# Mixture of experts: every expert over every row, or 39 routed tiles of 256 rows

## The reference, cut to what matters

```python
x = x + tanh(g_xattn[1]) * _L1_xattn_ref(ctx, _layernorm(x), ...)   # attention with 16 heads of 64, keys = x's and ctx's rows
x = x + tanh(g_ffn[1]) * _L1_ffn_ref(_layernorm(x), Wg, W1, W2, W3)

def _L1_ffn_ref(x, Wg, W1, W2, W3):            # E = 8 experts, K = 2, H = 256
    gate_out = einsum('bsd,ed->bse', x, Wg)
    top_v, top_i = top_k(gate_out, K)
    probs = softmax(top_v)
    out = zeros_like(x)
    for e in range(E):
        w_e = sum(probs * (top_i == e), axis=-1)
        h1, h2 = x @ W1[e].T, x @ W2[e].T
        out = out + ((h1 * sigmoid(h1) * h2) @ W3[e].T) * w_e[..., None]
    return out
```

## Time and profile before

| | |
|---|---|
| profiled execution, its own time | 1409.91 us |
| its span, first to last instruction | 1407.9 us |
| mean granted TensorE clock | 0.887 |
| PE, DVE, ACT, POOL busy | 1186.7, 1085.4, 931.6, 903.1 us |
| attention of layer 1 | about 475 to 1068 us |
| mixture | about 1105 to 1408 us |
| DMA, mean over the span | 26 GB/s |

### The profile page before, as it was taken

One profiled execution on the slowest core, in us unless ns is written; L12 is line 12 of the kernel. 1 busy time (PEld: TensorE's weight loads), 2 busy tenths in 40 slices (PEclk: granted clock), 3 DMA queues, 4 the chain that ended last, 5 costly groups with the idle time before them and its releaser, 6 DMA issues. The chain is left out here.

```text
span 1407.9 us, 39161 instructions
## 1 busy us (share of the span) xinstructions
PE 1186.7 (84%) x14613; PEld 889.4 (63%) x14613; DVE 1085.4 (77%) x2846; ACT 931.6 (66%) x1858; POOL 903.1 (64%) x855
## 2 busy tenths in 40 slices
PE   1578999949874699999999999999994688888887
PEld 1445777734542488888887878787873355555555
DVE  5888888867868666767767676868675799998996
ACT  0668999936655488787887878787872455454554
POOL 0250999945767366676666666666663477777778
PEclk9669555559995799999999999999997799999999
DMA  9100000001220011111111211112111000000000
GB/s 228 55 1 1 13 16 16 16 10 27 42 53 1 1 32 32 32 32 32 25 32 32 32 25 32 32 32 30 31 29 23 1 2 9 8 7 7 7 8 16
DMA packets 121437, 37.30 MB, mean 26 GB/s; under 512 B 105876, under 2 KB 119612, under 8 KB 121276
## 3 DMA queue, kind: packets, MB, share of 16 engines
q1 hardware_dynamic: 110235, 31.70, 10.8%
q10 hardware_dynamic: 11040, 3.42, 1.0%
HBM read 9.92 MB, written 2.10 MB: 9 GB/s over the span
## 5 line engine op out<-in xcount | busy, mean ns | idle before, releaser
L1178 POOL TENSOR_TENSOR attention_pl_l<-attention_probs_l,attention_ph_l 128x512 f16<-128x512 f32 x128 | 148.4, 1159 | 180.3 <-ACT attention_ph_l L1348 180.3
L1412 DVE TENSOR_REDUCE attention_negmax<-bank 128x2 f16<-128x410 f32 x256 | 137.7, 579 | 136.3 <-PE bank L1257 136.0
L1594 POOL TENSOR_TENSOR mixture_hidden_l<-mixture_hidden,mixture_hidden_h 128x512 f16<-128x512 f32 x128 | 148.4, 1160 | 74.8 <-ACT mixture_hidden_h L1681 74.8
L612 POOL TENSOR_TENSOR attention_probs_l<-attention_probs,attention_probs_h 77x512 f16<-77x512 f32 x128 | 145.5, 1153 | 52.7 <-ACT attention_probs_h L694 48.5
L1178 POOL TENSOR_TENSOR attention_pl_c<-attention_probs_c,attention_ph_c 77x512 f16<-77x512 f32 x128 | 147.8, 1155 | 0.0
L1690 ACT ACTIVATE mixture_tanh<-bank 128x512 f32<-128x512 f32 x128 | 76.4, 597 | 105.3 <-PE bank L1641 105.3
L1639 PE MATMUL bank<-mixture_xs,moeh 128*128 128x512 f16 x256 | 98.2, 383 | 32.0 <-DVE mixture_hidden L1772 32.0
L1272 PEld LDWEIGHTS bank<-identh,attention_negmax 128*128 128x128 f16 (+1 forms) x1024 | 83.3, 107 | 55.7
L1240 PE MATMUL bank<-layer_kv,ah 128*128 128x128 f16 x1024 | 108.7, 220 | 11.1 <-PEq L89 11.0
L1348 ACT ACTIVATE attention_probs_l<-bank 128x512 f32<-128x512 f32 x128 | 76.4, 597 | 56.8 <-PE bank L1272 56.8
L1268 PE MATMUL bank<-attention_th,layer_kv 128*128 128x512 f16 (+1 forms) x256 | 97.0, 379 | 14.7 <-issue 14.5
(11 more groups left out here) (323 smaller groups left out, 4788.0 us busy)
## 6 DMA issues: line engine op xcount, KB each, us to landing
X<-in_x SPq DMA_DIRECT2D x4, 512.0 KB, 9.2
out<-X SPq DMA_DIRECT2D x8, 256.0 KB, 2.3
attention_turned_h<-attention_heads_h SPq DMA_TRANSPOSE x96, 2.3
attention_turned_l<-attention_heads_l SPq DMA_TRANSPOSE x96, 2.3
ctx<-in_ctx SPq DMA_DIRECT2D x1, 1232.0 KB
setup_nat_w<-in_w SPq DMA_DIRECT2D x1, 1024.0 KB, 14.6
setup_nat_f<-in_fw ACTq DMA_DIRECT2D x2, 256.0 KB, 6.9
setup_nat_q<-in_q ACTq DMA_DIRECT2D x1, 512.0 KB, 8.3
```

What stands on the lines that cost most here:

```text
L612: pool.tensor_tensor(probs_l[:, n % SLOTS], probs[:, n % 2], probs_h[:, n % SLOTS], ALU.subtract).then_inc(p_split, 1)
L1178: last = pool.tensor_tensor(low[:, g % 2], whole[:, g % 2], high[:, g % 2], ALU.subtract)
L1412: last = dve.tensor_reduce(negmax[:, g, 2 * i:2 * i + 2], score[i], AX.X, ALU.max, negate=True)
L1594: pool.tensor_tensor(hidden_l[:, e % 4, j], hidden[:, e % 2, j], hidden_h[:, e % 4, j], ALU.subtract).then_inc(hid_lo, 1)
```

## The change

**Setup.** A DRAM tensor `tokens` of ROWS = 34560 rows of 272 fp16 (544 bytes) is written once with a blank row by one DMA that SP issues last in its setup block. POOL makes some constants more.

**Attention 1.** The routing of each batch k of four sequences is spread over later sequences, on fixed places (`ending(b, lag)` gives k where b = 4k + lag): reciprocal roots on POOL by the power function and one Newton step (lag 6 for the output, 7 for X), normed rows on ACT, a packed row of high half, low half and its number (`pay`, lag 7 to 8), four DMA transposes and one copy on SP, gates on PE (lag 9), the two largest and their indices on DVE, the choice on POOL, the rank of each row within its expert on PE (lag 10), the slot on DVE and POOL (lag 11), and then eight indirect DMAs by POOL, one per unit, that scatter 128 rows each into `tokens`. The stage runs `B + 14` turns, the last 14 without attention. DVE then makes a table of 39 tiles.

**Experts.** 39 tiles of 256 rows of one expert each. Their number is a constant: (2 * 4096 + 8 * 255) // 256. SP loads and transposes a tile from DRAM, ACT fetches the row numbers, PE, ACT and DVE work as before but with 256 rows, POOL scatters the results to `outputs` in DRAM with two indirect DMAs per tile. Then both results of each row are read back, and DVE adds them to X with their shares.

```diff
+T = 256
+ROW = 2 * 128 + 16
+TILES = (2 * B * S + E * (T - 1)) // T
+ROWS = E * B * S + (TILES - 2 * B * S // T) * T
@@ setup, sync
+            sp.wait_ge(blank_in, 1)
+            sp.dma_start(w.tokens.rearrange("(t p) r -> p t r", p=128),
+                         w.blank[:].unsqueeze(1).broadcast_to([128, ROWS // 128, ROW])).then_inc(w.cleared, 16)
@@ attention1, gpsimd
+            def row_scale(i, var, mean, eps):
+                y, z = rstd[:, i], shift[:, i]
+                link(pool.tensor_scalar(part[:], var, eps, None, ALU.add))
+                link(pool.tensor_tensor(y, part[:], power[:], ALU.pow))
+                for _ in range(1):
+                    link(pool.tensor_tensor(z, y, y, ALU.mult))
+                    link(pool.tensor_tensor(z, z, part[:], ALU.mult))
+                    link(pool.tensor_scalar(z, z, -0.5, 1.5, ALU.mult, ALU.add))
+                    link(pool.tensor_tensor(y, y, z, ALU.mult))
+                link(pool.tensor_scalar(z, mean, -1.0, None, ALU.mult))
+                return pool.tensor_tensor(z, z, y, ALU.mult)
+            def fill(k):
+                pool.wait_ge(pay_hi, k + 1)
+                pool.iota(...)
+                pool.tensor_tensor(pay[:, u, 0, :, D:2 * D], normed_x, pay[:, u, 0, :, 0:D], ALU.subtract).then_inc(pay_lo, 1)
+            def select(k):
...
+                link(pool.tensor_copy(chosen[:], index[:, :, 0:2]))
+                for i in range(2):
+                    for c in range(BATCH):
+                        last = pool.tensor_scalar(is_it[:, i, c], w.iota[:], chosen[:, c, i:i + 1], None, ALU.is_equal)
...
+            def send(k, q):
...
+                pool.indirect_dma_start(w.tokens, bass.IndirectOffsetOnAxis(ap=slot[:, u, i, c:c + 1], axis=0),
+                                        pay[:, u, i, c], None).then_inc(sent[u], 16)
@@ attention1, sync
+            def rows(k):
...
+                sp.wait_ge(pay_lo, k + 1)
+                for c in range(BATCH):
+                    sp.dma_start_transpose(rows_t[:, u, c], pay[:, u, 0, c, 0:2 * D]).then_inc(turned_x[u], 16)
...
+                sp.dma_start(pay[:, u, 1, :, 0:2 * D], pay[:, u, 0, :, 0:2 * D]).then_inc(doubled[u], 16)
@@ attention1, tensor: in project(t)
+                k = ending(t, 7)
+                if k is not None:
+                    pe.wait_ge(topped, 2 * k + 1)
+            def choose(k):
+                pe.wait_ge(turned_x[u], 16 * BATCH * (k // 2 + 1))
...                                                        # 16 matmuls of 8 columns
@@ attention1, vector
+            def top_two(k):
+                dve.wait_ge(gated, k + 1)
...
+                dve.tensor_copy(gate[:].rearrange("p c e -> p (c e)"), gates).then_inc(topped, 1)
-            def guess(k):
-            def newton(k, i):
-            def out_norm(k):
@@ experts
+            for n in range(TILES):                          # sync
+                row = sp.value_load(w.table[0:1, 0, n:n + 1], min_val=0, max_val=ROWS - T)
+                if n >= RX:
+                    sp.wait_ge(h_done, n - RX + 1)
+                sp.dma_start_transpose(xt[:, n % RX], w.tokens[bass.ds(row, T), 0:2 * D]).then_inc(x_in[n % RX], 16)
+            back = w.outputs.rearrange("(b s i) d -> s b i d", s=S, i=2)
+            for k in range(NCH):
+                sp.dma_start(both[:, k % RB], back[:, CH * k:CH * k + CH]).then_inc(both_in[k % RB], 16)
+            for n in range(TILES + LAG + 1):                # scalar
+                if n < TILES:
+                    squash(n)
+                if 1 <= n < TILES + 1:
+                    hidden_high(n - 1)
+                if n < TILES:
+                    number(n)                               # value_load and a DMA of the row numbers
+                if n >= LAG + 1:
+                    copy_out(n - LAG - 1)
+            for n in range(TILES + 1):                      # vector
+                if n < TILES:
+                    halve(n)
+                    hide(n)
+                if n >= 1:
+                    hidden_low(n - 1)
+            def send(n):                                    # gpsimd
+                pool.wait_ge(y_copied, n + 1)
+                pool.wait_ge(id_in[n % RI], 16 * (n // RI + 1))
+                for r in range(T // S):
+                    pool.indirect_dma_start(w.outputs, ..., y_rows[:, n % RY, r], None, ...).then_inc(y_out[n % RY], 16)
@@ flamingo
+                nc.clear_and_free_semaphores(w.spent)
+                nc.all_engine_barrier()
                 attention1(nc, w, bank, kv)
-            split_transposed(nc, w, bank, "split2", [...], before=row_scale(w))
-            mixture(nc, a, w, bank, xh, xl)
+        nc.clear_and_free_semaphores(w.spent)
+        nc.all_engine_barrier()
+        experts(nc, a, w, bank)
```

More of the change, by code:

```diff
@@ L1152, in attention1, with unit, ending @@
         out_p = bank[7][:, 0:D]
+        gates = bank[7][:, 128:128 + E * BATCH]
+        rank = bank[7][:, 256:256 + E * BATCH].rearrange("p (c e) -> p c e", e=E)
+        count = bank[7][:, 384:384 + E]
         LAT, CTX = slice(0, S), slice(S, KV)
         VALUES_AHEAD = 3
[L1157 to L1161, removed]
+        UNITS = B * G
+        BATCHES = B // BATCH
+        ROUTED = 14
+        def unit(n):
+            return (n // G, n % G, n // G % 2)
+        def ending(b, lag):
+            k, rest = divmod(b - lag, BATCH)
+            return k if rest == 0 and 0 <= k < BATCHES else None
         def sequences(body):
-            for b in range(B):
-                body(b, b % 2, b == 0, b == B - 1)
+            for b in range(B + ROUTED):
+                body(b)
         def batch(k):
@@ L1212, in body @@
                         add_bias(k)
[L1213 to L1216, removed]
+                    k = ending(b, 6)
+                    if k is not None and g == 0:
+                        out_scale(k)
+                    if k is not None and g == 2:
+                        gain(k)
+                        residual(k)
+                    k = ending(b, 7)
@@ L1218, in _ @@
+                    if k is not None and g == 1:
+                        count_up(k)
+                    for q in range(2 * BATCH):
+                        k = ending(b - (2 + q) // G, 11)
+                        if k is not None and g == (2 + q) % G:
+                            send(k, q)
+            link(pool.memset(power[:], -0.5))
+            pool.memset(pay[:, :, :, :, 2 * D + 2:ROW].rearrange("p u i c r -> p (u i c) r"), 0.0).then_inc(padded, 1)
             sequences(body)
-            heads_low(B - 1, 1)
@@ L1236, in _, with body @@
+            def body(t):
+                if t < B:
+                    if t >= 2:
+                        sp.wait_ge(projected, t - 1)
+                    for half in range(2):
+                        heads(t, half)
+                k = ending(t, 7)
+                if k is not None:
+                    rows(k)
+            sequences(body)
         @block.tensor
@@ L1385, in body @@
                         heads_high(b, 0)
-                    if not (last and g + 2 >= G):
-                        t_high(*after(b, g, u, 2))
-                    if not (last and g > 0):
-                        values_out(*after(b, g, u, VALUES_AHEAD))
+                    if n + 2 < UNITS:
+                        t_high(*unit(n + 2))
+                    if n + VALUES_AHEAD < UNITS:
+                        values_out(*unit(n + VALUES_AHEAD))
+                    k = ending(b, 6)
+                    if k is not None and g == 1:
+                        out_norm(k)
@@ L1815, in flamingo @@
+            for n in range(TILES):
+                send(n)
 def flamingo(nc, a):
```

799 lines of the change are left out of this document (442 added, 357 removed).

## The result

The changed kernel takes 1360.6 us (1360.0 to 1362.0, four runs) beside 1410.5 for the kernel before (1409.5 to 1411.5, four runs). The ratio is 0.965, 95% interval 0.964 to 0.966: 50 us are gained where 127 were forecast, and the time lies outside the range of 1242 to 1345. The direction was right, the size was not.

The account below looks back on a forecast made before the run. PE was taken to bound the attention (97% busy), PE and DVE the mixture (89 to 90%). Terms 0 + 7 + 3 + 18.4 - 155.1 = -126.7 gave span 1281, median 1284 us; range 1242 to 1345.

Parts of the forecast that it names:

- Setup, 0: Setup: the 18.8 MB clearing DMA, issued by SP on an empty queue, and POOL's new constants cost 0.
- Attention, removed and new wait: Attention: PE's waits behind small DVE operations go, -14.0 us; project waits for `topped` in six sequences, 6 x 2.5 = +15.
- Attention, POOL: Attention: POOL's new operations and eight indirect DMAs per batch fit, 65 of 73 us busy, so they cost 0.
- Each insertion is under the 1.8 us: Attention: each new piece of POOL work is shorter than the 1.8 us POOL waits for ACT anyway.
- some 2 us more: Attention: further slack of some 2 us after POOL's wait before PE needs POOL's result.
- The estimate of 1.0 us a send beside the forecast: POOL's indirect DMAs: an alternative price from the Trainium skill's first-byte time, 1.0 us instead of the forecast's 1.2.
- The tail, 41: Between attention and experts: batch 7's routing chain, 35.3, hops 3, and 3 for batch 6's DMAs on POOL, 41 us.
- The experts: Experts' loop: a tile takes the slowest engine, ACT at about 2.6, plus hops, 2.8 us; 39 tiles are 109.
- rival C: Experts: slow clock, or register loads on PE per tile; at clock 0.50 a tile costs 3.9, +43, 1327; chance 0.15.
- Rival A: Indirect DMAs make POOL the bound; saving gone at p = 2.5 us; chance 0.03 above that, 0.07 between 1.8 and 2.5.
- Read-back, 25: After the last tile: reading 4 MB at 234 GB/s 18, latency 2.3, last additions 2, store 2.3: 25 us.

Follow-up runs that it names:

- one_send: Changed kernel with only the first of each tile's two indirect DMAs issued and the buffer zeroed in setup by a second plain DMA; 1374.6 us, ratio 0.974.
- gates_early: Changed kernel with VectorE's copy of the gates out of bank 7 moved from the end of unit g=1 to g=0; 1346.8 us, ratio 0.955.
- sends_later: Changed kernel with each of a batch's eight sends in attention 1 one unit later in GpSimd's order; 1357.0 us, ratio 0.962.
- plain_pool: Changed kernel with the experts' 78 indirect DMAs issued by POOL as plain DMAs to consecutive rows; 1318.8 us, ratio 0.936.
- best2: Changed kernel with attention sends later, gates copied early, y copied first, tail sends in POOL's pauses, and a 128x128 addition behind each experts' send; 1313.6 us.

## Why the prediction was wrong, step by step

*Setup, 0.* Right (+1.2). `one_send` supports the reason, the empty queue: a smaller DMA issued behind the moving one held SP 64 us.

*Attention, removed and new wait.* Right: 12.4 of the 14.0 us went, and the wait for `topped` cost 13.0 of 15; `gates_early` took exactly that away.

*Attention, POOL: "I take 0".* Wrong, 16.2 us (18.2 less the 2.0 that the kernel before had). The price of an indirect DMA was right (0.97 us and a gap of 0.30; 1.27 forecast as 1.2), and the sum over a batch too: POOL is 80% busy. The error was to compare the batch's total with the batch's idle time. "Each insertion is under the 1.8 us" did not hold for the root, which was put down as 2.0 and takes 3.1, since the power takes 1.04 us and the seven small operations stand 0.28 us apart. With the "some 2 us more" that the forecast allowed it still fits when it is alone, but the root, the slot cast and a send stand in one unit and do not. `sends_later` shows it: with the root apart from the send, PE waits at most 0.8 us at a time in the stream. (The estimate of 1.0 us a send beside the forecast took a time to the first byte for a time of POOL; a send costs POOL 1.27 here.)

*The tail, 41.* Short by 10. The largest part is at its end: from the last send's end (1152.77) to SP's first transpose 8.9 us pass, where landing and barrier were put down as 3.8, so 5.1 more. The two roots are 2.1 over; from the last index (1137.80) to the end of the choice 3.0 us pass, where 1.9 stood. The rest, some 2 us, is spread over norming, transposes, slot and sends. One wait came as forecast: fill(7) starts at 1128.05 although ACT's cast ended at 1124.83, because four sends stand ahead of it in POOL's order. That is 3.2 us, and the sum had 3 for it. Both, in the timeline:

```profile
1124.20 0.63 ACT L1607 ACTIVATE attention_pay<-ctx 128x512 f16<-128x512 f32 x1
1124.55 0.96 POOL L1322 DMA_INDIRECT tokens<-attention_pay,attention_slot  x1 [0.31 <-issue]
1125.81 0.96 POOL L1322 DMA_INDIRECT tokens<-attention_pay,attention_slot  x1 [0.30 <-issue]
1127.07 0.96 POOL L1322 DMA_INDIRECT tokens<-attention_pay,attention_slot  x1 [0.30 <-issue]
1128.05 0.16 POOL L1274 IOTA attention_pay<- 128x8 int32 x1
...
1151.82 0.95 POOL L1322 DMA_INDIRECT tokens<-attention_pay,attention_slot  x1 [0.30 <-issue]
1161.70 7.37 SPq L1855 DMA_TRANSPOSE experts_xt<-tokens  x4
```

What fills the 8.9 us (landing, clearing of semaphores, barrier, register load) was not taken apart.

*The experts, "a tile takes the slowest plus hops: 2.8".* This step failed, and with it the forecast: a tile took 4.10 us. The slowest engine was named wrongly, which is 0.3 us of the error. ACT was put first with 2.6 and PE down for 1.97, half an old period; PE takes 1.48 + 0.98, each from its first matmul's start to its last one's end, and the gaps of two register loads, of which rival C had spoken, bring it to 3.0 and the tile to 3.09. The other 1.0 us a tile is the hold, a wait that the sum did not have. `plain_pool` puts it at 41.8 us; without it the time would lie inside the range. The sum counted the sends as POOL's time only; nothing in the trace of before could show what they do to TensorE's updates, as it had no indirect DMA. None of the rivals held it. Rival A had the right instruction and the wrong mechanism: the price of one was as forecast. Rival C's clock did not decide: in `plain_pool` it is 1.00 from 1180 to 1280, in the changed kernel 0.88, where TensorE waits more. A slip stands in rival A: by its own prices p = 2.7 ends at 1442 and not at 1415; nothing else was taken from it.

*Read-back, 25.* Measured 28.5. The 18 us in it came out near by luck: they were priced as 4 MB at 234 GB/s, but the reads ran at 286 GB/s from 1336 to 1357, and what fills the time is VectorE, whose 64 additions of 347 ns stand end to end. Beside them, the last send ends 3.0 us behind the last copy, and 3.7 us pass from SP's issue to the first addition.

```profile
L1962 DVE SCALAR_TENSOR_TENSOR X<-experts_both,share,X 128x128 f32<-128x128 f32 x64 | 17.6, 347 | 16.0 <-DMA experts_both<-outputs 15.7
```

## What to carry to other kernels

Fit inserted work unit by unit, not by the batch's total: two insertions that each fit into an idle stretch cost their sum where they meet. When every engine is half idle in a steady loop, compare the end of the producer with the update time of its semaphore before looking for a missing buffer; a "remote" wait on a semaphore of the core's own engine is the sign. And leave room between indirect DMAs issued by GpSimd when TensorE's results are waited for: a pause that costs GpSimd 0.36 us a send bought 0.6 us a tile.

## What the runs showed of the hardware

- Indirect DMAs issued by GpSimd 1.29 us apart hold TensorE's semaphore updates, those of `rise` by up to 2.8 us in the changed kernel. From rise's end to tanh it takes 1.42 us there on average, 0.35 with the sends 1.65 us apart (`best2`), and 0.04 with one send every 3 us (`one_send`). Plain DMAs from GpSimd hold none, though two of them stand only 0.53 us apart, nor do those of SP. Of VectorE's 101 updates in the loop of the changed kernel 90 were seen within 0.02 us, and for the other 11 the trace has no update near. Why it is so no run shows; the plain DMAs also write to consecutive rows, so the indirect form and the scattered places are not told apart. The Trainium skill (Perfetto Trace Analysis, DMA Instruction — SWDGE (GPSIMD)) says that the bar of such an instruction ends when the last descriptor is written and not when data have moved. The trace agrees: the send that ended at 1240.38 had its updates at 1241.48 to 1241.68, and the held updates of 1241.31 and 1241.45 come just ahead of them.
- Where nothing is held, an update is seen 0.01 to 0.02 us behind the modelled end of its matmul; in the changed kernel the waiting tanh starts 1.42 us behind it on average. The Trainium skill (TensorE: Matmul & The Clock Gate, The cost: per-tile semaphore tail) puts some 26 ns on each semaphore update in its formula for matmuls packed side by side into the array. No run here has such a packing; the 0.01 to 0.02 us above are of that size, and the hold is a case of which the formula does not speak.
- One DMA of 34560 rows of 544 bytes is issued in 0.41 us on an empty queue; in `one_send` the next one, issued 0.05 us behind it, holds SP for 64 us.
- TensorE fell from 2.4 to 1.2 GHz for 3.4 us behind five of the six waits before project (2.15 us each) in `sends_later`, and behind none of these in the changed kernel, which differs only in POOL's order. The changed kernel has one such stretch in the attention, behind a wait for POOL, and `gates_early` two (at 701.1 and 929.8). What decides is open.
